# First attention of a four-layer kernel: values' products, keys and positions as 64x64 tiles in float32

## The reference, cut to what matters

```python
kv = jnp.concatenate([memory, layer_input], axis=1)
q = (layer_input @ Wq).reshape(b, q_len, n_head, d_head)
k = (kv @ Wk).reshape(b, kl, n_head, d_head)
v = (kv @ Wv).reshape(b, kl, n_head, d_head)
r = (pe @ Wr).reshape(kl, n_head, d_head)
ac = jnp.einsum('bqhd,bkhd->bhqk', q + content_bias, k)
bd = rel_shift(jnp.einsum('bqhd,khd->bhqk', q + position_bias, r))
scores = (ac + bd) * (1.0 / np.sqrt(d_head))
attn = jax.nn.softmax(scores, axis=-1)
ctx = jnp.einsum('bhqk,bkhd->bqhd', attn, v).reshape(b, q_len, n_head * d_head)
out = layer_norm(layer_input + ctx @ Wo, ln1_g, ln1_b)
```

## Time and profile before

| | us |
|---|---|
| median of 3 runs | 1943.75 (1938.99 to 1948.05) |
| profiled execution, time | 1940.73 |
| its span | 1939.2 |
| granted TensorE clock over the span | 0.904 of full |
| stretch of the first attention's loop, 60 to 580: clock | 1.00 |

### The profile page before, as it was taken

The page is one execution under the profiler, slowest core; times in us unless marked ns, Lnnn a source line. Parts: engine busy times, 40 slices in busy tenths (PEclk is TensorE's granted clock), DMA queues, the critical chain, the costliest instruction groups (busy, mean ns, idle before and its releaser), DMA issues. The chain is left out here.

```text
span 1939.2 us, 54781 instructions
## 1 busy us (share of the span) xinstructions
PE 1621.0 (84%) x17114; PEld 1295.5 (67%) x17114; DVE 1329.5 (69%) x4084; ACT 1199.0 (62%) x3451; POOL 946.9 (49%) x1389
## 2 busy tenths in 40 slices
PE   6999999999996869999999775479998884448981
PEld 5888888888884747667777662157776664437771
DVE  3777777777775638888777536668887883337772
ACT  2776777677674426677777335468888771137771
POOL 3354344444441454556665434534454444646773
PEclk8999999999998979999999787579999995559996
DMA  9676666766662022221000000000000000136765
GB/s 240 150 155 139 157 148 137 162 141 151 149 146 58 1 92 107 94 105 43 19 18 11 1 1 1 0 4 1 0 10 13 12 9 23 44 110 213 215 212 155
DMA packets 214819, 167.06 MB, mean 86 GB/s; under 512 B 27632, under 2 KB 188784, under 8 KB 214448
## 3 DMA queue, kind: packets, MB, share of 16 engines
q1 hardware_dynamic: 206128, 142.75, 29.1%
q0 software_dynamic: 8576, 22.88, 3.6%
HBM read 91.79 MB, written 73.76 MB: 85 GB/s over the span
## 5 line engine op out<-in xcount | busy, mean ns | idle before, releaser
L738 ACT ACTIVATE sb_probs<-sb_probs,sb_work 128x128 f32<-128x128 f32 x512 | 198.6, 406 | 120.3 <-DVE sb_work L641 120.3
L281 POOL TENSOR_SCALAR sb_next_var_eps<-sb_next_moments 128x1 f32<-128x1 f32 (+1 forms) x184 | 45.3, 246 | 433.2 <-DVE sb_next_moments L721 246.6
L890 POOL TENSOR_TENSOR sb_work<-sb_work,sb_cols 128x512 f32<-128x512 f32 x128 | 134.2, 1048 | 215.6 <-ACT sb_work L1107 133.6
L1033 DVE TENSOR_REDUCE sb_work<-PS 128x8 f32<-128x512 f32 x256 | 175.3, 685 | 46.9 <-PE PS L932 44.5
L1035 DVE TENSOR_TENSOR sb_work<-PS,sb_work 128x512 f32<-128x512 f32 x256 | 177.1, 692 | 8.8
L1067 ACT ACTIVATE sb_work<-sb_work 128x512 f32<-128x512 f32 x256 | 161.6, 631 | 33.4 <-DVE sb_work L1035 27.5
L906 PE MATMUL PS<-sb_ident,sb_work 128*128 128x128 f32 x1024 | 150.0, 287 | 15.9 <-ACT sb_work L1107 10.6
L959 PEld LDWEIGHTS PS<-sb_v_ones,sb_work 128*64 128x64 f32 x4096 | 133.0, 140 | 24.7 <-issue 16.9
L959 PE MATMUL PS<-sb_v_ones,sb_work 128*64 128x18 f32 x4096 | 144.9, 214 | 4.6 <-ACT sb_work L1073 2.8
L1073 ACT ACTIVATE sb_work<-PS 128x512 f32<-128x512 f32 x256 | 139.7, 594 | 10.1 <-PE PS L906 6.8
L906 PEld LDWEIGHTS PS<-sb_ident,sb_work 128*128 128x128 f32 x1024 | 113.8, 145 | 43.5 <-issue 31.3
(11 more groups left out here) (281 smaller groups left out, 4467.1 us busy)
## 6 DMA issues: line engine op xcount, KB each, us to landing
rel_scratch<-sb_work SPq DMA_DIRECT2D x64, 516.0 KB, 7.3
sb_work<-rel_scratch SPq DMA_DIRECT2D x64, 512.0 KB, 6.6
expert_rows<-sb_blank SPq DMA_DIRECT2D x36, 520.0 KB, 2.9
sb_w_up<-expert_halves SPq DMA_DIRECT2D x23, 512.0 KB, 3.6
sb_w_down<-expert_halves SPq DMA_DIRECT2D x23, 512.0 KB, 3.4
expert_halves<-sb_e_halves POOLq DMA_DIRECT2D x16, 512.0 KB, 6.2
sb_work<-expert_rows SPq DMA_DIRECT2D x23, 260.0 KB, 3.3
sb_e_raw<-e_W POOLq DMA_DIRECT2D x16, 256.0 KB, 5.3
```

Source lines behind the costliest of these rows:

```text
L738: ins = e.activation(probs[:, j], probs[:, j], ACT.Exp, bias=neg_max[:, j:j + 1], scale=-1.0, accum_out=row_sum[:, j:j + 1])
L890: e.tensor_tensor(k_masked[:, u3], k_sb[:, u3].rearrange("p (b k) -> p b k", b=2).unsqueeze(2) .to_broadcast([P, 2, 4, S]), col("place").u ...
L1033: e.tensor_reduce(top, mine, AX.X, ALU.max).then_inc(sem("att_max_ready"), 1)
```

## The change

- Each float32 product of L536 and L555, and each key product, becomes four products of 64x64 weights: the upper and lower half of the rows (of the contraction) times the left and right half of the columns. The function `half_product(e, r, ...)` issues the two of one row half `r`. The two row halves never write the same bank at the same time: in the product of probabilities and tokens, each bank gets one half in a first phase and the other in a second, with a semaphore (`l0_pkv_half`) between; the values' table's halves go to banks 3 and 0 and are added on DVE in two additions; the keys go bank by bank in pairs, (1, 2), (0, 3), then (2, 1), (3, 0), with the semaphore `l0_k_half`.
- The position rows (L572) are issued for each sequence alone, as products of 64x64 weights.
- The keys are computed in float32 from `w_k0` and `kvT`. The split, its buffers, `x_own` and the three products of each key go. The queries read `kvT` with a step.
- The first pair of the keys comes before the position rows, the other three behind them.
- The transposed probabilities use the banks in the order 1, 2, 0, 3, and DVE copies the last two banks one by one. The tokens' transposes wait for all of these copies.
- On DVE, the tokens' copy and the pooled sum come behind one `add_relative` and not two.
- Some semaphores in later layers are merged, with no instruction moved.

```diff
+        TURN = (1, 2, 0, 3)
+        HALVES = (slice(0, P // 2), slice(P // 2, P))
+
+        def half_product(e, r, o, left, right, **flags):
+            for x in HALVES:
+                ins = e.matmul(o[x], left[HALVES[r], x], right[HALVES[r]], skip_group_check=True, **flags)
+            return ins
...
                     if has(0):
-                        e.wait_ge(sem("l0_probsT_kept"), 2 * n + 1)
+                        e.wait_ge(sem("l0_probsT_kept"), 2 * n + 2)
...
-                    for j in range(4):
-                        G, b = j // 2, j % 2
-                        e.wait_ge(sem("l0_probsT_kept"), 2 * n + (1 if j == 0 else 2))
-                        if j == 3 and has(3):
-                            e.wait_ge(sem("l0_kv_kept"), 2 * (n + 3) + 2)
-                        e.matmul(PS[:, (j + 1) % 4], kv_in[:, u, b], probsT[:, 8 * G:8 * G + 8, S * b:S * b + S],
-                                 start=True, stop=True).then_inc(sem("l0_pkv_done"), 1)
+                    for phase in range(2):
+                        for G in range(2):
+                            if phase:
+                                wait_alone(e, sem("l0_pkv_half"), 2 * n + G + 1)
+                            else:
+                                wait_alone(e, sem("l0_probsT_kept"), 2 * n + G + 1)
+                                if G and has(3):
+                                    wait_alone(e, sem("l0_kv_kept"), 2 * (n + 3) + 2)
+                            for r in range(2):
+                                b = (r + phase) % 2
+                                ins = half_product(e, r, PS[:, (2 * G + b + 1) % 4], kv_in[:, u, b],
+                                                   probsT[:, 8 * G:8 * G + 8, S * b:S * b + S],
+                                                   start=(phase == 0), stop=(phase == 1))
...
-                        ins = e.matmul(PS[:, 3, 0:D], pkvT[:, j], VO[:, j], start=(j == 0), stop=(j == H - 1))
+                        for r in range(2):
+                            ins = half_product(e, r, PS[:, (3, 0)[r], 0:D], pkvT[:, j], VO[:, j],
+                                               start=(j == 0), stop=(j == H - 1))
...
+                    def keys(r, bank, first):
+                        for i in range(2):
+                            at = P * (2 * bank + i)
+                            ins = half_product(e, r, PS[:, bank, 2 * KL * i:2 * KL * i + 2 * KL], w_k0[:, at:at + P],
+                                               kvT[:, :], start=(first and i == 0), stop=not first)
+                        return ins
+
+                    wait_alone(e, sem("l0_q_kept"), 2 * t + 2)
+                    keys(0, 1, True)
+                    keys(1, 2, True).then_inc(sem("l0_k_half"), 1)
...
-                                ins = e.matmul(PS[:, 4 + g, i * KL:i * KL + KL], q0T[r, v3, ch], rT[r, ch],
-                                               start=True, stop=True, skip_group_check=True)
+                                for b in range(2):
+                                    ins = e.matmul(PS[S * b:S * b + S, 4 + g, i * KL:i * KL + KL],
+                                                   q0T[r, v3, ch, S * b:S * b + S], rT[r, ch],
+                                                   start=True, stop=True, skip_group_check=True)
...
-                            ins = product_in_parts(e, PS[:, j, 2 * KL * i:2 * KL * i + 2 * KL],
-                                                   (w_k0_hi[:, at:at + P], w_k0_lo[:, at:at + P]),
-                                                   (x_hi0[:, :], x_lo0[:, :]))
-                        ins.then_inc(sem("l0_k_done"), 1)
+                    wait_alone(e, sem("l0_kv_kept"), 2 * t + 2)
+                    keys(0, 0, True)
+                    keys(1, 3, True).then_inc(sem("l0_k_half"), 1)
+                    wait_alone(e, sem("l0_k_half"), 2 * t + 1)
+                    keys(0, 2, False)
+                    keys(1, 1, False).then_inc(sem("l0_k_done"), 2)
+                    wait_alone(e, sem("l0_k_half"), 2 * t + 2)
+                    keys(0, 3, False)
+                    keys(1, 0, False).then_inc(sem("l0_k_done"), 2)
...
                     e.wait_ge(sem("l0_kvT_done"), t + 1)
-                    e.tensor_copy(x_own.rearrange("p (b q) -> p b q", b=2),
-                                  transposed.rearrange("p (b a k) -> p a b k", b=2, a=2)[:, 1])
-                    e.tensor_copy(x_hi0[:, :], transposed).then_inc(sem("l0_kv_kept"), 1)
+                    e.tensor_copy(kvT[:, :], transposed).then_inc(sem("l0_kv_kept"), 1)
...
-                    e.wait_ge(sem("l0_kv_kept"), 2 * t + 1)
-                    e.tensor_tensor(x_lo0[:, :], transposed, x_hi0[:, :].bitcast(F32), ALU.subtract)\
                         .then_inc(sem("l0_kv_kept"), 1)
                 if has(1):
+                    add_relative(1)
                     add_relative(2)
                     add_relative(3)
```

More of the change, by code:

```diff
@@ L327, in build @@
         rel_shifted = carve((H, KL))
-        x_own = carve((P,))
+        half_added = carve((D,))
         mask_f = carve((KL + 1,))
@@ L577, in step @@
-                    for j in range(4):
-                        if j == 0 and has(0):
-                            e.wait_ge(sem("l0_pkvT_kept"), 4 * n + 4)
-                        elif 1 <= j <= 2:
-                            e.wait_ge(sem("l0_q_kept"), 2 * t + j)
-                        elif j == 3 and has(0):
-                            e.wait_ge(sem("l0_out_added"), n + 1)
-                        elif j == 3 and has(2):
-                            e.wait_ge(sem("l0_k_kept"), 4 * (n + 2) + 4)
-                        for i in range(2):
-                            at = P * (2 * j + i)
-                            ins = product_in_parts(e, PS[:, j, 2 * KL * i:2 * KL * i + 2 * KL],
-                                                   (w_k0_hi[:, at:at + P], w_k0_lo[:, at:at + P]),
-                                                   (x_hi0[:, :], x_lo0[:, :]))
-                        ins.then_inc(sem("l0_k_done"), 1)
+                    if has(0):
+                        wait_alone(e, sem("l0_out_added"), n + 1)
+                    elif has(2):
+                        wait_alone(e, sem("l0_k_kept"), 4 * (n + 2) + 4)
@@ L660, in step @@
                 if has(0):
[L661 to L664 removed]
+                    e.wait_ge(sem("l0_probsT_done"), 4 * n + 2)
+                    e.tensor_copy(probsT[:, 0:8].rearrange("p (g i) k -> p g (i k)", g=2), PS[:, 1:3])\
+                        .then_inc(sem("l0_probsT_kept"), 1)
+                    e.wait_ge(sem("l0_probsT_done"), 4 * n + 4)
+                    e.tensor_copy(probsT[:, 8:12].rearrange("p i k -> p (i k)"), PS[:, 0])
+                    e.tensor_copy(probsT[:, 12:16].rearrange("p i k -> p (i k)"), PS[:, 3])\
+                        .then_inc(sem("l0_probsT_kept"), 1)
                 if has(1):
@@ L667, in step @@
                     add_relative(0)
-                    add_relative(1)
                 if has(3):
@@ L768, in step @@
                     t = n + 3
-                    for j in range(4):
-                        e.wait_ge(sem("l0_k_done"), 4 * t + j + 1)
-                        e.activation(k0T[:, v3, 2 * j:2 * j + 2], PS[:, j].rearrange("p (i k) -> p i k", i=2), ACT.Copy)\
+                    for j, bank in enumerate(TURN):
+                        e.wait_ge(sem("l0_k_done"), 4 * t + 2 * (j // 2) + 2)
+                        e.activation(k0T[:, v3, 2 * bank:2 * bank + 2], PS[:, bank].rearrange("p (i k) -> p i k", i=2), ACT.Copy)\
                             .then_inc(sem("l0_k_kept"), 1)
@@ L1588, in route_tensor @@
             e.wait_ge(sem("routing"), routed("carry", NQ))
-            e.matmul(PS[:, 3, 0:NE], all_ones, carry[:, NQ % 2], start=True, stop=True).then_inc(sem("moe_counted"), 1)
+            e.matmul(PS[:, 3, 0:NE], all_ones, carry[:, NQ % 2], start=True, stop=True).then_inc(sem("moe_prefix_done"), 1)
         def route_vector(e, c):
```

67 lines of the change are left out of this document (31 added, 36 removed).

## The result

| | before | after |
|---|---|---|
| median of the runs side by side, us | 1945.9 | 2111.57 (2099.05 to 2124.03, 4 runs) |
| ratio, 95% interval | | 1.0856 (1.0819 to 1.0893) |
| profiled execution: time, span, us | 1940.73, 1939.2 | 2107.97, 2106.4 |

A forecast was written before the change was run, and what follows sets the result against it. PE, full at 520.00 of 520 us, and a ring of PE and DVE waits were both taken to bound the 17.85 us step. 32 tiles x 0.91 = 29.1 on 1940.7 gave 1970 us, range 1953 to 1992.

The forecast's parts named there:

- PE's own sum: First attention's loop: PE's instruction prices added up, 17.85 us before, 18.53 after (+0.68); as a rival alone, 1963 us, chance 0.15.
- Groups of four at 0.215 for 256 columns, 0.43 for 512: Four side-by-side 64x64 rows: 0.215 us a group in keys, 0.43 in probabilities times tokens.
- Values' table 3.5 to 3.6, positions 1.76: Tiled products in the loop: values' table 3.5 to 3.6 us a step, positions 16 groups at 0.11 us.
- The rival of bursts: Keys: second product for a busy tile delays lower tiles by 0.43 us; +1.54 a step, 1990 us, chance 0.15.
- the ring: Loop of mutual waits between PE and DVE: 17.85 us before, 18.76 after, +0.91 a step; chance 0.48.
- A wait of PE for the pooled sum: Before the second quarter of tokens times probabilities, PE waits about 0.2 us for DVE's pooled sum in each step.
- about when the queries end: ACT gets its first `pkvT` bank some 1.3 us later and finishes its copies about when PE's queries end.
- A granted clock under 1.00 would be wrong: Sign against the forecast: PE's granted clock falling under 1.00 in the first attention's stretch.
- the sum 1969.8: Whole kernel: profiled execution 1940.7 plus 29.1 us (32 tiles at 0.91); given as 1970 us.

The follow-up runs named there:

- run 1: Changed kernel with TensorE's loop body cut from four steps to two, tokens loaded twice into alternating buffers; 2009.49 us, ratio 1.0339.
- experiment 3: Kernel before with a TensorE loop body of eight steps in place of four, no work changed; 1948.38 us, ratio 1.0039.
- run 6: Kernel before with a loop body of two steps in place of four and the tokens loaded twice; 1941.57 us, ratio 1.0003.
- run 4: Kernel before with only the values' table in 64x64 tiles, two additions on DVE, loop of four steps; 1984.85 us, ratio 1.0224.
- run 10: Kernel before with values' table and position rows in 64x64 tiles, fp32r keys as before, loop of two steps; 1950.27 us, ratio 1.0072.
- run 8: Changed kernel with the values' table back on the full array, loop of two steps; 1983.09 us, ratio 1.0211.
- run 9: Changed kernel with values' table and tokens' product back on the full array, loop of two steps; 1962.62 us, ratio 1.0149.
- run 7: Changed kernel with the values' table back on the full array, loop of four steps; 2014.36 us, ratio 1.0360.

## Why the prediction was wrong in size

**Where the 167 us are.** The span grew by 167.2 us. Steps n = 0 to 28 of the changed kernel take 678.1 us together, 160.4 over 29 steps of 17.85. Of these, 29 x 1.13 = 33 are what a step takes without holes (18.98, run 1). The holes over 0.4 us are 38, 89.5 us together. The stretch of these steps in one line shows both them and the clock:

```profile
61.10:739.19 678.09, 588.41 (x11198) 466.40 (x11195) 383.85 (x1537) 359.32 (x1393) 231.84 (x266) 0.96 0.52 115
```

PE is busy 588.41 of 678.09 us, and a mean clock of 0.96 in place of 1.00 is 27 us: the clock is at its lower level, half of the upper, for 54.6 us in all, behind 16 of the 38 holes. So such a hole costs 1.7 us more, and the other 22 cost nothing by the clock. Of the 11 us that are left, some 6 are, by an estimate from experiment 3, the 0.15 us at the last row before each hole; 5 are not accounted for. The remaining 7 us of the span lie before step 0 and behind step 28.

**The step that failed** is in the part on PE's own sum: "So four 64x64 rows side by side cost what one full row costs, and splitting a product into four gives nothing and takes nothing." As a price of streams it held. But it was taken as the whole price: the sum counted columns, and nowhere instructions, though the diff and the order of instructions both told that a step issues 384 more of them. Nor did I list a lack of instructions among the rivals. The earlier trace rows even had the warning's other half, a PE that was never idle in the stretch and at full clock, so that any hole adds fully and can take the clock too.

The mechanism, as the runs show it: a full-array row with its load is two instructions in 0.11 us, four tiles in the same 0.11 us are eight. The values' table in tiles uses 256 instructions in 3.54 us, the full array 64 in 3.67. The Trainium skill (Runtime: NRT & Kernel Launch, Instruction fetch mechanics) says that TensorE's instruction memory holds 2048 instructions, refilled in order by blocks of 256, and that a taken branch to a block outside the sequencer's window, which it puts at two blocks, has to wait for a fetch. The traces agree in the size of a block (16384 bytes a packet, holes at multiples of 256 instructions), in the loops (bodies of at most 1552 matmuls and weight loads, 1637 with the sequencer's own instructions, leave 12 to 19 packets between 60 and 580 us; bodies of 2320, 2409 in all, and more leave 51 to 76), and in the wait at the way back (experiment 3, 3.02 us). They don't agree with a window of two: the kernel before goes back over 1637 instructions without a hole and without a packet. The same section says that crossing a block is mostly hidden. By runs 3 and 6 this holds for the kernel before; by runs 1, 4 and 10 it does not hold for tiles of 128 columns in code that is fetched as it runs.

**Point by point.**
- *Groups of four at 0.215 for 256 columns, 0.43 for 512:* right. The first pair of the keys is 0.86 for four groups (367.96 to 368.82 in run 1), the other three pairs 2.75 with the switch to transposes. Keys 3.61 in all, against 3.44 and a switch.
- *Values' table 3.5 to 3.6, positions 1.76:* right, 3.54 and 1.75.
- *The rival of bursts* (two products to a busy tile hold up the others): refuted. In run 1's first key pair the lower tiles start 0.06 us behind the upper ones and not 0.43. The rule of the Trainium skill that spoke for it (TensorE: Matmul & The Clock Gate, Part 3), that matmuls start and end strictly in program order, gave the wrong size here: tiles work on side by side two products deep.
- *PE's own sum 18.53, the ring 18.76:* near. Without holes a step takes 18.98. By runs 1, 8 and 9 the +1.13 over 17.85 is 0.81 for keys and positions with the switches around them (forecast 0.61 and 0.11), 0.40 for the tokens' product in two phases (forecast: a share of the ring's 0.23), and -0.08 for the values' table.
- *A wait of PE for the pooled sum:* wrong. No such wait stands in the list. The late phases moved it to the queries, which wait for ACT's copies of `pkvT` (8.9 us in 11 times in run 1). I had written that ACT ends them "about when the queries end"; what decides is the first of its copies, which the queries' banks need. How the 0.40 divides between this wait and the switches of form was not settled.
- *A granted clock under 1.00 would be wrong:* this is what came, 0.96, and each stretch at the lower clock lies behind a hole.
- *Two slips that decide nothing:* the sum 1969.8 was one for the profiled execution, so that the median should have been given as 1973 and not 1970; and PE did idle before the stretch, up to 5.77 us at a time (44.8 to 50.6 us).

**What stays open.** Why the packet of the next block starts between 0.2 and 9.2 us (mostly 1.2 to 5.1) after the block before it has been entered, and what passes in the 1.2 to 1.8 us between its landing and PE's going on. At the two ways back of experiment 3 this second time is 2.3 and 2.4 us. Whether data transfers hold up the fetch was not tried.

## What to carry to other kernels

Count instructions as well as columns: before a product is split into tiles, work out how many microseconds 256 of TensorE's instructions will last in the densest stretch, and whether a loop's body stays loaded (1552 instructions did here, 2320 did not). In the changed kernel each block used up in 4.2 to 4.4 us was followed by a hole, and of 44 that lasted 6.2 to 8.3 us, 2 were. If a body does not fit, shorten the loop first; that alone was worth 100 us of the 166 here. And a change to an engine that never idles has to be priced with the clock: of two idle times of 3 us in one run, one cost 4.5 us with the lower clock behind it, and the other, with one of 0.45 behind it, 4.0 without.

## What I had not expected of the hardware

- Idle time of TensorE for lack of instructions, up to 4.3 us at a time, shown in the profile only as "issue", at borders of 256 instructions; it ends 1.2 to 1.8 us after an instruction packet has landed.
- The way back of a loop longer than what is held: 3.02 and 3.06 us, with 4.5 and 4.0 lost in all. The two kernels with 2320 instructions in their loop (experiments 4 and 7) show 1.9 to 2.6 us there.
- 25 KB of instructions in each step of 17.85 us (388 of 64 bytes, experiment 3) are hidden, but for the ways back; the changed kernel, with 50 KB in about 19 us, has up to two holes a step.
